# Feeding the network with unturned features, bit checks in one product, and an earlier filter chain

## What is computed

```python
xn = layernorm(x)                                  # x: 8192 tokens x 256
D = fractal_dimension(xn)                          # from the first 1024 elements of xn
filt = wave_filter(D, 256)
x1 = ifft(fft(xn) * filt).real                     # a circulant 256 x 256 product
bits = sigmoid(x1 @ W_el + b_el) > 0.5             # 24 bits a token
syn = bits @ H.T > 0.5                             # 12 checks, any overlap counts
w = syn.sum(-1)                                    # bits 0..2 of the pattern, if 0 < w <= 3
corrected = where(do_fix, mod(bits + pattern, 2), bits)
out = x + x1 + corrected @ W_le + b_le + gelu(xn @ w1 + b1) @ w2 + b2
```

## Time and profile before

| | us |
|---|---|
| median of 3 runs | 441.99 (441.98 to 442.23) |
| the profiled execution | 442.09 |
| its span | 440.3 |
| TensorE busy in it | 423.0 (96%) |
| VectorE, ScalarE, GpSimd busy | 277.2, 193.5, 76.3 |

### The profile page before, as it was taken

One profiled execution on the slowest core, in us unless ns is written; L12 is line 12 of the kernel. 1 busy time (PEld: TensorE's weight loads), 2 busy tenths in 40 slices (PEclk: granted clock), 3 DMA queues, 4 the chain that ended last, 5 costly groups with the idle time before them and its releaser, 6 DMA issues.

```text
span 440.3 us, 5676 instructions
## 1 busy us (share of the span) xinstructions
PE 423.0 (96%) x1832; PEld 335.2 (76%) x1832; DVE 277.2 (63%) x534; ACT 193.5 (44%) x306; POOL 76.3 (17%) x116
## 2 busy tenths in 40 slices
PE   6996989999999999999999999999999999999993
PEld 3774768787887878888787888878788878878872
DVE  5964558575757557565756757575666748565445
ACT  3841533444534444453544445353444535354430
POOL 2066102021120302112030212103021210300000
PEclk9998899999999999999999999999999999999999
DMA  8554122332303233320223333122233301011011
GB/s 234 159 148 140 7 91 96 96 97 79 100 14 95 95 96 97 95 94 8 94 91 96 95 96 95 12 103 76 96 95 96 95 33 56 7 48 49 0 48 48
DMA packets 18141, 35.97 MB, mean 82 GB/s; under 512 B 7385, under 2 KB 9681, under 8 KB 18130
## 3 DMA queue, kind: packets, MB, share of 16 engines
q1 hardware_dynamic: 18130, 35.84, 26.4%
HBM read 27.38 MB, written 8.45 MB: 81 GB/s over the span
## 4 chain that ended last, share of the span: by engine, by line
PE 90%; DVE 4%; POOL 2%; ACT 1%; issue 1%; DMA 1%; DVEq 0%; POOLq 0%
PE p_h L797 38%; PE p_f L815 25%; PE p_f L820 13%; PE p_s L852 5%; PE p_l L841 5%; PE p_s L870 2%; PE p_g L864 1%; PE p_g L860 1%; DVE h_lo L533 1%; DMA x_sb<-L_attn_x 1%; PE p_l L929 0%; POOL row_nums L337 0%; DVE flips L547 0%; POOL wave L383 0%; POOL wave L370 0%
## 5 line engine op out<-in xcount | busy, mean ns | idle before, releaser
L411 ACT ACTIVATE h<-p_h,b_sb 128x512 f32<-128x512 f32 x128 | 88.2, 689 | 211.1 <-PE p_h L797 202.8
L533 DVE TENSOR_TENSOR h_lo<-h,h_hi 128x512 fp32r<-128x512 f32 x128 | 88.3, 690 | 72.2 <-ACT h_hi L419 71.7
L815 PE MATMUL p_f<-h_hi,w_hi 128*128 128x512 f32 x254 | 108.0, 425 | 0.0
L815 PE MATMUL p_f<-h_hi,w_lo 128*128 128x512 f32 x254 | 99.2, 391 | 0.0
L419 ACT CAST h_hi<-h 128x512 fp32r<-128x512 f32 x128 | 79.5, 621 | 5.8
L797 PE MATMUL p_h<-xT_hi,w_hi 128*128 128x512 f32 (+1 forms) x258 | 81.1, 396 | 0.1
L797 PE MATMUL p_h<-xT_lo,w_hi 128*128 128x512 f32 (+1 forms) x258 | 80.0, 392 | 0.0
L797 PE MATMUL p_h<-xT_hi,w_lo 128*128 128x512 f32 (+1 forms) x258 | 79.9, 391 | 0.0
L820 PE MATMUL p_f<-h_lo,w_hi 128*128 128x512 f32 x254 | 78.5, 390 | 1.4 <-DVE h_lo L533 1.4
L815 PEld LDWEIGHTS p_f<-h_hi,w_hi 128*128 128x128 f32 x254 | 47.8, 188 | 13.5
L797 PEld LDWEIGHTS p_h<-xT_hi,w_hi 128*128 128x128 f32 x258 | 48.8, 192 | 11.3 <-DVE w_lo L640 0.6
(11 more groups left out here) (119 smaller groups left out, 337.4 us busy)
## 6 DMA issues: line engine op xcount, KB each, us to landing
xt_sb<-xt SPq DMA_DIRECT2D x16, 512.0 KB, 5.4
x_sb<-L_attn_x SPq DMA_DIRECT2D x15, 512.0 KB, 4.7
rows_sb<-rows_dram SPq DMA_DIRECT2D x15, 512.0 KB, 4.5
out<-xt_sb SPq DMA_DIRECT2D x15, 512.0 KB, 2.9
w_f<-L_ffn_w SPq DMA_DIRECT2D x3, 512.0 KB, 7.0
x_sb<-L_attn_x SPq DMA_DIRECT2D x2, 256.0 KB, 2.9
w_f<-L_ffn_w SPq DMA_DIRECT2D x2, 256.0 KB, 5.5
basis_sb<-basis SPq DMA_DIRECT2D x1, 384.0 KB, 3.4
```

The costliest lines, as they stand in the source:

```text
L411: nc.scalar.activation(h[m % 2][:], p_h[:, m % 2, :], ACT.Gelu, bias=b1_sb[:, m:m + 1]).then_inc(gelu_done, 1)
L533: nc.vector.tensor_tensor(h_lo[m % HR][:], h[m % 2][:], h_hi[m % HR][:].bitcast(F32), ALU.subtract).then_inc(h_lo_done, 1)
L815: mm(p_f[:, a, :], w[:, m, a * HF:(a + 1) * HF], h_hi[r][:], start=(m == 0 and w is w2_hi), stop=False, skip_group_check=True)
```

## The change

1. The network reads normalised features that are not turned. `w1` isn't turned any more. `xn` is a buffer of its own; `centre` and `scale` are one instruction each over both halves (128x1024), as is the split (`columns_hi`, `columns_lo`). GpSimd's `turn` reads the normalised chunk and writes `uv`; a second split makes `uv_hi` and `uv_lo` (`turned_hi`, `turned_lo`), which only `filtered` reads.
2. `latents` takes four products: one weight tile `cw` carries the high parts of the latent weights in columns 0 to 23 and the low parts in columns 32 to 55. ScalarE copies the low columns' result, negated, to `rest`; `take_bits` compares. It runs in the chunk's own turn, not one chunk later.
3. `checks` replaces `count` and `weigh`: one product over a word that holds the bits of this and of the previous chunk, a row of ones and the previous checks. `correct` is one compare on the bit pattern of the result.
4. The prefix elements are copied from the transposed chunk 0 in PSUM (`fr_v`), with the tables of constants laid out to fit, in place of the way through DRAM. The series is evaluated in pairs; ScalarE weighs the basis. The steps on VectorE, ScalarE and TensorE in chunk 0 are laid out anew: `circulant` stands behind `down(0, 4)`, `latent_weights` behind `down(0, 6)`.
5. The first chunk of x is loaded in three pieces (128, 128 and 256 KB); the identity is its own load, the small arrays are packed on the host into two; `w1` and `w2` are loaded into the space of late chunks. The last piece but one of the output is issued by ScalarE.

```diff
-W1_PARTS = ((0, 2), (2, 4), (4, MB))
-W2_PARTS = ((0, 4), (4, MB))
+W1_PARTS = ((0, 2), (2, 4), (4, 6), (6, MB))
+W1_LOADS = ((0, 2), (2, 4), (4, MB))
+W2_PARTS = ((0, 2), (2, 4), (4, MB))
+W2_LOADS = ((0, 4), (4, MB))
...
-            for cols, arrived in ((slice(0, HALF * E), x_head), (slice(HALF * E, CW), x_in[0])):
+            for cols, arrived in ((slice(0, E), x_first[0]), (slice(E, HALF * E), x_first[1]),
+                                  (slice(HALF * E, CW), x_in[0])):
...
-            sp.wait_ge(xn_done, 1)
-            sp.wait_ge(xn_head, 1)
-            sp.dma_start(head_dram.unsqueeze(0), xn[0:1, :, :].rearrange("o a e -> o (a e)")).then_inc(fr_out, 16)
-            sp.wait_ge(fr_out, 16)
-            sp.dma_start(fr_v[:, :], head_dram.rearrange("(p f) -> p f", f=FRE)).then_inc(fr_in, 16)
...
+            def turn(c, first=False):
+                if first:
+                    pool.wait_ge(xc0_made, 1)
                 else:
-                    pool.wait_ge(t_lo, KB * c)
+                    pool.wait_ge(scaled, c)
+                    pool.wait_ge(u_lo, c)
+                columns = xc0 if first else xn
+                for k, op in enumerate((ALU.add, ALU.subtract)):
+                    nc.gpsimd.tensor_tensor(uv[:, k, :], columns[:, 0, :], columns[:, 1, :], op).then_inc(turned, 1)
...
+            turn(0, first=True)
+            inverse_root(2 + HEAD, 0)
+            turn(1)
...
+            def latents_rest(c, first=False):
+                act.wait_ge(lat_done, c + 1)
+                if not first:
+                    act.wait_ge(bits_done, c)
+                nc.scalar.mul(rest[:], p_l[SEG:SEG + LAT, :], -1.0).then_inc(rest_done, 1)
...
+            gelu(0, 6, first=True)
+            hidden_hi(0, 6, first=True)
+            act.wait_ge(basis_in, 16)
+            act.wait_ge(filt_made, 1)
+            for k in range(KB):
+                nc.scalar.mul(basis_w[:, k, :], basis_sb[:, k, HF:HF + E], filt_w[:, k:k + 1]).then_inc(basis_wd, 1)
+            gelu(0, 7, first=True)
+            hidden_hi(0, 7, first=True)
+            act.wait_ge(c_made, 1)
+            made = p_l[:, 0:E].rearrange("p (a e) -> p a e", a=2)
+            nc.scalar.copy(c_f[:, :, :], made).then_inc(c_copied, 1)
+            nc.scalar.copy(c_hi[:, :, :], made).then_inc(c_hi_ready, 1)
+            act.wait_ge(cw_made, 1)
+            act.wait_ge(cw_set, 1)
+            nc.scalar.copy(cw[:, :, 0:LAT], latent_made).then_inc(cw_hi_ready, 1)
+            columns_hi(1, 1)
+            turned_hi(0, first=True)
...
             def chunk(c, par):
                 b = c - 1
                 statistics(c + 1, 1 - par)
                 add_ffn(b)
                 dve.wait_ge(stats_made, c + HEAD + 2)
                 hidden_lo(c, 0)
                 aggregate(1 - par)
-                take_bits(b)
+                take_bits(c, par)
                 hidden_lo(c, 1)
-                take_checks(b)
+                turned_lo(c)
                 hidden_lo(c, 2)
                 correct(b)
+                take_checks(c)
                 hidden_lo(c, 3)
                 centre(c + 1, 1 - par)
                 scale(c + 1, 1 - par)
                 hidden_lo(c, 4)
-                dve.wait_ge(le_done, c)
-                dve.wait_ge(ffn_added, KB * c)
                 add_sums(b)
+                columns_lo(c + 1, 1 - par)
                 hidden_lo(c, 5)
                 add_differences(b)
-                turned_lo(c + 1, 1 - par, 0)
                 hidden_lo(c, 6)
-                turned_lo(c + 1, 1 - par, 1)
                 hidden_lo(c, 7)
...
+            def chunk(c, par):
+                b = c - 1
                 for m in range(MB):
                     up(c, par, m)
                     if m == 0:
-                        latents(b, bpar)
+                        latents(c, par)
                     if m == 1:
-                        filtered(b, bpar)
-                    if m == 2:
-                        count(b)
-                    if m == 3:
-                        weigh(b)
-                    if m == 5:
-                        le_products(b)
+                        filtered(b)
                     if m >= 2:
                         down(c, m - 2)
+                    if m == 2:
+                        checks(c, par)
+                    if m == 4:
+                        le_products(b)
...
+            def first_branch_chunk(c, par):
+                b = c - 1
+                for m in range(MB):
+                    up(c, par, m)
+                    if m == 0:
+                        pe.wait_ge(c_ready, 1)
+                        latents(b, 1 - par, first=True)
+                    if m == 2:
+                        latents(c, par)
+                        filtered(b, first=True)
+                    if m >= 2:
+                        down(c, m - 2)
+                    if m == 2:
+                        pe.wait_ge(code_ready, 1)
+                        pe.wait_ge(word_set, 3)
+                        checks(b, 1 - par)
+                    if m == 4:
+                        checks(c, par)
+                    if m == 5:
+                        pe.wait_ge(le_ready, 2)
+                        le_products(b)
...
             def last_chunk(c, par):
...
+                    if m == 4:
+                        le_products(b)
+                        checks(c + 1, 1 - par)
                     if m == 7:
-                        filtered(c, par)
-                        count(c)
+                        filtered(c)
+                        le_products(c)
                 down(c, MB - 2)
-                weigh(c)
-                le_products(c)
                 last_down(c, MB - 1)
...
             for m in range(LOOK):
                 up(0, 0, m, first=True)
+                if m == 2:
+                    summed_over(0, NS, fr_s[:, 0, :], part_sums, fr_summed)
             for m in range(MB):
                 down(0, m, first=True)
+                if m == 0:
+                    summed_over(8, NS, fr_s[:, 2, :], part_counts, fr_counted)
                 if m == 1:
-                    summed_over(0, NS, fr_s[:, 0, :], part_sums, fr_summed)
-                if m == 2:
-                    summed_over(8, NS, fr_s[:, 2, :], part_counts, fr_counted)
-                if m == 3:
                     summed_over(16, 1, fr_d[:, 0:1], logged, dim_made)
+                if m == 4:
+                    circulant()
+                if m == 6:
+                    latent_weights()
                 if m + LOOK < MB:
                     up(0, 0, m + LOOK, first=True)
-            circulant()
-            latent_weights()
-
-            chunk(1, 1, first_branch=True)
+            first_branch_chunk(1, 1)
```

More of the change, by code:

```diff
@@ L1 @@
 import math
+import struct
 from contextlib import ExitStack
@@ L48, with build @@
 K_INVN = K_NUM + FRE
[L49 to L55, removed]
+K_C1 = K_INVN + NS
+K_C2 = K_C1 + COLS
+K_ODD = K_C2 + COLS
+K_EVEN = K_ODD + PAIRS * COLS
+K_WK = K_EVEN + PAIRS * COLS
+K_END = K_WK + COLS
+S_B1 = 0
+S_BLE = S_B1 + MB
+S_B2 = S_BLE + KB
+S_WEL = S_B2 + KB
+S_END = S_WEL + KB * LAT
+def build(nc, x, xt, small, latent, w1, w2, ident, consts, basis, codes, out):
     ctx = ExitStack()
@@ L424, in chunk @@
                     hidden_hi(c, m)
-                    if m >= 5 and m < 7 and not last:
-                        turned_hi(c + 1, 1 - par, m - 5)
+                    if m == 0:
+                        latents_rest(c)
+                    if m == 1:
+                        turned_hi(c)
+                    if m == 4:
+                        columns_hi(c + 1, 1 - par)
+            def first_branch_chunk(c, par):
+                for m in range(MB):
+                    gelu(c, m)
+                    hidden_hi(c, m)
+                    if m == 0:
+                        latents_rest(c - 1, first=True)
+                    if m == 2:
+                        latents_rest(c)
+                        turned_hi(c)
+                    if m == 4:
+                        columns_hi(c + 1, 1 - par)
@@ new lines, in _ @@
+            for g in range(2):
+                act.wait_ge(t0_done, g + 1)
+                nc.scalar.copy(half_tokens(xT_hi[0], g), half_bank(g)).then_inc(t0_hi, 1)
+            w1_part_hi(1)
+            act.wait_ge(small_in, 16)
+            gelu(0, 0, first=True)
+            hidden_hi(0, 0, first=True)
+            w2_part_hi(0)
+            gelu(0, 1, first=True)
+            hidden_hi(0, 1, first=True)
+            w1_part_hi(2)
+            gelu(0, 2, first=True)
+            hidden_hi(0, 2, first=True)
@@ new lines, in _ @@
+            w2_part_hi(1)
+            w1_part_hi(3)
+            gelu(0, 3, first=True)
+            hidden_hi(0, 3, first=True)
+            w2_part_hi(2)
+            act.wait_ge(fr_taken, 1)
+            for g in range(2):
+                last = nc.scalar.copy(half_tokens(xc0, g), half_bank(g))
+            last.then_inc(xc0_made, 1)
+            gelu(0, 4, first=True)
```

(4 more changed lines are left out.)

708 lines of the change are left out of this document (362 added, 346 removed).

## The result

The changed kernel takes 418.95 us in the median of 4 runs (418.89 to 419.05), against 441.99 before (441.90 to 442.23): a ratio of 0.948 (0.946 to 0.950), 23 us less. The profiled execution took 418.89, with a span of 417.1. The forecast was 418.4.

The account below looks back on a forecast made before the run. TensorE's count of products times their pace bounds steady chunks; the head has waits and a lower clock. 442.09 - 8.9 (steady chunks) - 9.6 (head) - 3.7 (last chunk) - 1.4 (tail) = 418.5, so 418.4 against the median; range 414.5 to 424.8.

Parts of the forecast that it names:

- Steady chunks: Chunks 2 to 14: 112 to 109 TensorE products at 0.228 us, 25.52 to 24.84 each, 8.9 us gained over 13 chunks.
- the term that the prediction bounded by 0 and 0.4 us a chunk: Added work and new order on the other engines in a steady chunk: 0 to 0.4 us a chunk, taken as 0.
- The 7.4 us in hand: In a steady chunk, columns_lo ends near 17.4 us and the next chunk's first up needs it at 24.84.
- the mutual delay: In steady chunks VectorE and GpSimd hold each other up: centre to columns_lo could each lose one GpSimd instruction.
- Rival 2: In steady chunks turn and the 128x1024 steps push a hidden_lo past its down: 0.4 us a chunk, 424.0; chance 0.12.
- The head: From the start to chunk 2's beginning: 72.4 to 62.8, 9.6 us gained (bounds 5 and 13).
- the clock's term: In the head, the first 12 products at the lower clock would make all 1.2 us later; 0.6 was taken.
- The series itself: GpSimd's new filter series in chunk 0: 12 instructions, nine in a chain, 3.1 us, done at 24 (bound 27).
- The weighed basis: In chunk 0 ScalarE weighs the basis behind hidden_hi(6), done at 25.6, 2 us in hand before circulant at 27.6.
- rival 1: In the head the filter is late again and circulant waits: 3.7 us and about 1.7 for the clock, 423.8; chance 0.13.
- Last chunk and tail: Last chunk to TensorE's end 30.84 to 27.1 us, 3.7 gained; from there to the span's end 5.4 to 4.0, 1.4 gained.

## Why the prediction was right, and where it wasn't

*Steady chunks: right in mechanism, the size off by an eighth.* TensorE's order has no wait in them, and the three missing products are the gain. Their price was right. The traces show it as distances between the starts of groups, in the mean of the 13 chunks:

| in a steady chunk, us | before | after |
|---|---|---|
| `latents`, six and four products | 1.38 | 0.93 |
| two check products and one, each with what the six behind it take over 1.36 | 0.48 | 0.25 |
| `up(1)`, `up(2)`, `down(0)`, `down(1)`, 24 products that weren't touched | 5.46 | 5.54 |
| everything else | 18.20 | 18.20 |

The first two rows give 0.68, the forecast to the hundredth. The step that failed is the term that the prediction bounded by 0 and 0.4 us a chunk and put at nothing: the steady chunk lost 0.08 in 24 products that stand between and behind the removed ones, 13 x 0.08 = 1.0 of the missing 1.1. In one chunk each, first latent product, first of `up(1)`, first of `up(2)`, and the start behind `up(2)`, before:
```profile
201.32 0.39 PE L841 MATMUL p_l<-xT_hi,cw_hi 128*96 128x512 f32 x1
...
202.70 0.62 PE L797 MATMUL p_h<-xT_hi,w_hi 128*128 128x512 f32 x2
...
205.47 0.62 PE L797 MATMUL p_h<-xT_hi,w_hi 128*128 128x512 f32 x2
...
206.83 0.38 PE L860 MATMUL p_g<-bits,code 96*96 96x512 bf16 x1
```
and after:
```profile
187.89 0.63 PE L926 MATMUL p_l<-xT_hi,cw 128*128 128x512 f32 x2
...
188.82 0.63 PE L882 MATMUL p_h<-xT_hi,w_hi 128*128 128x512 f32 x2
...
191.60 0.63 PE L882 MATMUL p_h<-xT_hi,w_hi 128*128 128x512 f32 x2
...
192.99 0.40 PE L900 MATMUL p_f<-h_hi,w_hi 128*128 128x512 f32 x1
```
`up(2)` takes 1.39 for 1.36. When two latent products are added back it takes 1.36 again, and this is why adding them cost 0.43 and not 0.47. Why these groups run slower is open: no wait stands in them, the clock is 1.00, and moving `turn` changed nothing (24.91 a chunk as well).

*The 7.4 us in hand.* In a steady chunk that begins at 186.52, `columns_lo` ends at 205.2, 18.7 in, and the next chunk starts at 24.91: 6.2 in hand. The missing 1.2 is for the greater part the delay beside `turn` (2.18 instead of 1.22), which I had weighed and costed at nothing. The Trainium skill (SBUF — State Buffer, on the shared port pair) has it that a VectorE operation with two SBUF inputs and a GpSimd operation that reads SBUF exclude each other for a whole instruction. The pair of lines for the split agrees: 0.96 us is lost, of a `turn` instruction of 1.48. The prediction had read the mutual delay from GpSimd instructions of different sizes (128x512 against 128x4), which doesn't show it; the run with the two apart does. Rival 2 needed the delay to reach TensorE through a `hidden_lo`: the one behind the split, `hidden_lo(5)`, ends at 205.84, and `down(5)` wants it at 208.25, so 2.4 us of room kept it away. A small misreading stands beside this: the chunk of the kernel before that the prediction put at 200.2 began at 199.95, so its `centre` stood 12.0 in, not 11.8; now it stands 12.1 in, where 11.3 was forecast and 0.3 allowed for the row numbers.

*The head: right in nearly every step.* First product 8.10 (forecast 8.3), `up(4)` at 16.59 with a wait of 0.46 (16.5, 0.6), the dimension's sum at 19.43 (19.5), `circulant` at 27.87 (27.6) for 0.68 to the next product (1.05), chunk 1's first product at 34.98 (35.1), then waits of 1.02 and 0.52 (1.3 and 1.1), chunk 2 at 61.98 (62.2 without the clock's term). The 0.8 that the term was too low are 0.6 for the clock, which wasn't lost at all (mean 1.00 up to 34.98), and 0.2 in chunk 1: the second wait was 0.6 shorter and the start 0.1 earlier, but the 114 products took 26.5, not 26.0. The series itself took 4.2 us, from 20.59 to 24.83, where 3.1 was forecast.

*One step was right by luck.* The weighed basis was forecast for 25.6, with 2 us of room. It came at 27.19:
```profile
23.18 0.42 ACT L516 ACTIVATE le<-le_t 24x256 bf16<-24x256 f32 x1 [2.53 <-DVE le_t L823]
...
26.28 0.91 ACT L526 ACTIVATE basis_w<-basis_sb,filt_w 128x256 f32<-128x256 f32 x2
```
ScalarE's `le3` copy waits 2.53 us for `le_t`, and every Gelu behind it waits too. I had walked TensorE's and VectorE's orders through this stretch, and ScalarE's without that step. 0.7 us of room were left. The run with 3 instructions more shows that the series itself had 1.3 of its own, and the one with 16 what lay beyond: there a wait of 5.42 made the profiled execution 7.5 longer, 2.1 beyond the wait, where rival 1 had counted 1.7 beyond its 3.7. The cause that nearly brought it was another one.

*Last chunk and tail* came as computed (27.18 for 27.1, 4.1 for 4.0), the tail in part by luck: the prediction had the pieces start when the first half is down, and they started behind the additions; the run that moved the branch shows the difference, 0.5 in the start of the pieces and 0.6 in the time.

*Parts of the head's 10.4.* The first product is 2.0 earlier (10.13 to 8.10); from there to chunk 1's first product 6.3 (33.16 to 26.88); chunk 1 itself 2.1 (29.11 to 27.00). The shortened series gave 3.4 of these in the old order; the place of the filter's products is worth 3.1 in the new one. These aren't shares of one sum: each holds while the other is in place. The earlier start, by the removed turning steps, the new DMA order and the smaller pieces together, wasn't taken apart but for the last. Nor does a run show what the unturned features (part 1 of the change) are worth in the steady chunks: they add work on VectorE and ScalarE there and take no product away.

## What to carry to other kernels

Where one engine is busy for a whole steady chunk, a count of instructions times their pace gives the gain of removing some, here 0.68 a chunk; but compare the groups that weren't touched as well, before you call the rest a wrong price. Here they took 0.08 of it back. Adding an instruction measures both together. Where a chain is moved under cover, write out the order of every engine on its way, also of the steps that only stand in front: here the cover held by 0.7 us, against 2 planned. And ask at the end of a chain, as at the last pieces here, which of two waits ends last; moving work that had no slack to lose gave another 0.4%.

## What the hardware did that I hadn't expected

- The clock: after waits of 1.02 and 1.43 us between full stretches it stayed at 2.4 GHz; after 0.46, eight small products and 2.49 it was 1.2 GHz from 38 to 41 us; after 3.74 and 5.42 the products behind the wait ran at 1.2 GHz. After the wait of 2.49 this cost 1.6.
- Two fp32r products of 512 columns added to a chunk took 0.47 in their place, but the chunk grew by 0.43; a bf16 one took 0.21, and the chunk grew by 0.19. Unchanged groups of six near them ran at 1.36 in one kernel and 1.39 in another, at full clock and without a wait.
- A small GpSimd instruction in a chain cost 0.28 us in one place and 0.47 in another of the same execution.
- The mutual delay of VectorE and GpSimd moved with the order: 2.18 for 1.22 on the split beside `turn`, or, with `turn` later, 773 ns for 704 on the mean `hidden_lo`.
